# A conditional residual layer: which masks are expanded on the chip, who copies them, when GpSimd splits x, and the store of the last half batch

## What is computed

```python
masked_w = weight * mask[None, :, :]                  # weight [G, O, T], mask [O, T]
w_bot = jnp.einsum('bg,got->bot', y, masked_w)        # y = cond_8 [B, G]
out = x + jnp.einsum('bnt,bot->bno', x, w_bot) + bias
```

## Time and profile before

| | |
|---|---|
| Median of 3 runs | 73.07 us (73.03 to 74.49) |
| The profiled execution, its own time | 72.25 us |
| Its span, first to last instruction | 70.1 us |
| TensorE (PE) busy | 61.8 us, 88% of the span |
| VectorE (DVE) busy | 51.2 us, 73% |
| ScalarE (ACT) busy | 45.0 us, 64% |
| GpSimd (POOL) busy | 10.7 us, 15% |
| Moved by DMA | 20.20 MB, 288 GB/s over the span |

### The profile page before, as it was taken

One profiled execution on the slowest core, in us unless ns is written; L12 is line 12 of the kernel. 1 busy time (PEld: TensorE's weight loads), 2 busy tenths in 40 slices (PEclk: granted clock), 3 DMA queues, 4 the chain that ended last, 5 costly groups with the idle time before them and its releaser, 6 DMA issues.

```text
span 70.1 us, 1524 instructions
## 1 busy us (share of the span) xinstructions
PE 61.8 (88%) x666; PEld 57.7 (82%) x666; DVE 51.2 (73%) x34; ACT 45.0 (64%) x35; POOL 10.7 (15%) x16
## 2 busy tenths in 40 slices
PE   3997898847999973999999999999999999999910
PEld 3873786736988843999999999999999999999900
DVE  2207988938748999999993999999999199460040
ACT  3300476818579992049999999999922999504500
POOL 5400059980349000000000000000000000000000
PEclk9999999999999999999999999999999999999996
DMA  0999999999630003999899999999899721998383
GB/s 1 241 298 382 409 423 449 397 430 280 248 164 0 0 0 126 416 332 220 353 435 435 400 435 376 386 348 283 271 395 376 297 115 61 402 409 339 136 313 150
DMA packets 4901, 20.20 MB, mean 288 GB/s; under 512 B 544, under 2 KB 800, under 8 KB 3872
## 3 DMA queue, kind: packets, MB, share of 16 engines
q1 hardware_dynamic: 4752, 20.06, 76.3%
q10 hardware_dynamic: 144, 0.07, 0.4%
HBM read 11.73 MB, written 8.39 MB: 287 GB/s over the span
## 4 chain that ended last, share of the span: by engine, by line
PE 64%; DVE 18%; DMA 7%; issue 3%; SPq 2%; ACT 2%; ACTq 0%
PE slots L311 19%; PE slots L313 19%; PE slots L312 19%; DVE w_raw L452 7%; DMA weights<-in_weight 7%; PE slots L286 7%; DVE w_lo L436 5%; DVE x_lo L430 3%; DVE weights L423 2%; ACT w_hi L362 2%; SPq L157 1%; PE slots L277 1%; DVE weights L446 1%; SPq L154 1%; ACTq L380 0%
## 5 line engine op out<-in xcount | busy, mean ns | idle before, releaser
L311 PE MATMUL slots<-x_hi,w_hi 128*128 128x256 f32 x112 | 31.3, 280 | 1.6 <-DVE x_lo L430 1.6
L312 PE MATMUL slots<-x_lo,w_hi 128*128 128x256 f32 x112 | 31.3, 279 | 0.0
L313 PE MATMUL slots<-x_hi,w_lo 128*128 128x256 f32 x112 | 31.3, 279 | 0.0
L311 PEld LDWEIGHTS slots<-x_hi,w_hi 128*128 128x128 f32 x112 | 21.0, 188 | 1.9 <-issue 1.9
L312 PEld LDWEIGHTS slots<-x_lo,w_hi 128*128 128x128 f32 x112 | 21.0, 188 | 0.0
L313 PEld LDWEIGHTS slots<-x_hi,w_lo 128*128 128x128 f32 x112 | 21.0, 188 | 0.0
L436 DVE TENSOR_TENSOR w_lo<-w_raw,w_hi 128x2048 fp32r<-128x2048 f32 (+1 forms) x8 | 17.3, 2174 | 1.2 <-ACT w_hi L362 1.2
L430 DVE TENSOR_TENSOR x_lo<-x_ring,x_hi 128x2048 fp32r<-128x2048 f32 x7 | 16.0, 2286 | 2.9 <-ACT x_hi L356 2.7
L356 ACT CAST x_hi<-x_ring 128x2048 fp32r<-128x2048 f32 x6 | 11.4, 1906 | 6.5 <-DMA x_ring<-in_x 6.5
L371 ACT ACTIVATE weights<-slots,smalls 128x1024 f32<-128x1024 f32 x11 | 11.8, 1113 | 3.5 <-PE slots L313 3.5
L377 ACT COPY w_raw<-slots 128x1024 f32<-128x1024 f32 x8 | 8.0, 1013 | 9.3 <-PE slots L286 9.3
(11 more groups left out here) (21 smaller groups left out, 16.1 us busy)
## 6 DMA issues: line engine op xcount, KB each, us to landing
x_ring<-in_x SPq DMA_DIRECT2D x8, 1024.0 KB, 9.3
out<-weights SPq DMA_DIRECT2D x15, 512.0 KB, 6.0
weights<-in_weight SPq DMA_DIRECT2D x3, 512.0 KB, 6.4
x_ring<-in_mask SPq DMA_DIRECT2D x2, 512.0 KB, 6.4
weights<-in_weight SPq DMA_DIRECT2D x2, 256.0 KB, 3.9
out<-weights SPq DMA_DIRECT2D x2, 256.0 KB, 2.2
few_masks<-in_few SPq DMA_DIRECT2D x1, 128.0 KB, 2.4
smalls<-in_small ACTq DMA_DIRECT2D x1, 65.0 KB, 2.6
```

Of the source, the lines that this page charges most:

```text
L311: nc.tensor.matmul(dst, wh, xh, start=(k == 0), stop=False)
L312: nc.tensor.matmul(dst, wh, xl, start=False, stop=False)
L313: last = nc.tensor.matmul(dst, wl, xh, start=False, stop=(k == KC - 1))
```

## The change

- The repeated masks that the host sends are now those of chunks 0 and 3 (`REPEATED = (0, 3)`); the expanded ones are those of chunks 1 and 2. The amount of data is the same.
- ScalarE issues the two halves of mask 0, around `smalls`. SP's order becomes few, weights 0 (two halves), weights 1, 2, 3, mask 3, x of group 0.
- TensorE expands mask 1 first, mask 2 in the middle of unit 0. ScalarE copies each to SBUF (`mask_by_act`), and the multiplications of chunks 1 (VectorE) and 2 (GpSimd) read it there. All four masks lie in slots 1 and 2 of `x_ring`, so x of group 1 is loaded only after `masked_by_dve` of 3 and `masked_by_pool` of 1, x of group 2 after `masked_by_pool` of 2.
- VectorE masks chunk 1 after it has copied its slot of unit 0; ScalarE copies both slots of unit 1. Unit 1 waits for the second mask copy instead of for the masks of chunk 1; unit 2 still waits for those, but only behind its four identity matmuls.
- GpSimd makes x_hi of group 1 between its second and third gather; VectorE makes x_lo of group 1 ahead of its two halves of w_lo.
- The last half, (7, 1): its fourth sample goes to a PSUM bank of its own (`very_last`). Its columns 0 to 511 are finished by ScalarE after two samples, 512 to 767 by VectorE after three, 768 to 1023 by ScalarE at the end, which also issues that last store.

The core of the diff:

```diff
+REPEATED = (0, 3)
...
+        def mask_of(c):
+            return x_ring[:, 1 + (c in REPEATED), (c // 2) * SLOT:(c // 2 + 1) * SLOT]
...
+        def raw_act(u):
+            return u + 1 + (u >= 1)
+        def raw_dve(u):
+            return u + 1 - (u >= 1)
...
 (SyncE)
-            sp.dma_start(weights[:, 1, :], weight[1]).then_inc(chunk_loaded[0], 16)
-            for c in range(BY_SPREAD, CHUNKS):
-                sp.dma_start(masks[:, c - BY_SPREAD, :], mask[c - BY_SPREAD]).then_inc(chunk_loaded[c - 1], 16)
+            for c in range(1, CHUNKS):
                 sp.dma_start(weights[:, c, :], weight[c]).then_inc(chunk_loaded[c - 1], 16)
-            for g in range(XS - 1):
-                load_group(g)
-            sp.wait_ge(masked_by_pool, CHUNKS - BY_SPREAD)
-            load_group(XS - 1)
+            sp.dma_start(mask_of(CHUNKS - 1), mask[1]).then_inc(chunk_loaded[CHUNKS - 2], 16)
+            load_group(0)
+            sp.wait_ge(masked_by_dve, 3)
+            sp.wait_ge(masked_by_pool, 1)
+            load_group(1)
+            sp.wait_ge(masked_by_pool, 2)
+            load_group(2)
...
 (GpSimd)
+            pool.wait_ge(chunk_loaded[1], 16)
+            pool.wait_ge(mask_by_act, 2)
+            nc.gpsimd.tensor_tensor(weights[:, 2, :], weights[:, 2, :], mask_of(2), ALU.mult).then_inc(masked_by_pool, 1)
+            pool.wait_ge(chunk_loaded[2], 32)
+            nc.gpsimd.tensor_tensor(weights[:, 3, :], weights[:, 3, :], mask_of(3), ALU.mult).then_inc(masked_by_pool, 1)
...
+            gather(0, 0)
+            gather(0, 1)
             pool.wait_ge(x_loaded[1], 16)
             nc.gpsimd.tensor_copy(x_hi[:, 1, :], x_ring[:, 1, :]).then_inc(x_hi_first, 1)
+            gather(1, 0)
+            gather(1, 1)
...
 (TensorE, unit u)
-                if u == 1 or u == 2:
-                    pe.wait_ge(masked_by_dve, 3)
+                if u == 1:
+                    pe.wait_ge(mask_by_act, 2)
...
+                if u == 2:
+                    pe.wait_ge(masked_by_dve, 3)
...
                 for q in range(QU):
+                    if u == 0 and q == 2:
+                        pe.wait_ge(mask_by_act, 1)
+                        spread_mask(1)
...
+                        if g == GROUPS - 1 and h == 1 and b == NB - 1:
+                            pe.wait_ge(out0_by_act, g)
+                            dst = very_last
...
 (ScalarE)
+            act.dma_start(mask_of(0)[:, 0:BANK], mask[0, :, 0:BANK]).then_inc(first_loaded[0], 16)
             act.dma_start(smalls[:], small).then_inc(smalls_loaded, 16)
+            act.dma_start(mask_of(0)[:, BANK:SLOT], mask[0, :, BANK:SLOT]).then_inc(first_loaded[1], 16)
...
+            for n in range(BY_SPREAD):
+                act.wait_ge(mask_spread, n + 1)
+                nc.scalar.copy(mask_of(n + 1).rearrange("p (q t) -> p q t", t=T), few_wide[:, :, n, :]).then_inc(mask_by_act, 1)
             for u in range(UNITS):
                 act.wait_ge(unit_ready, 2 * u + 1)
                 nc.scalar.copy(raw_slot(u, 0), slots[:, 2 * (u % 2), :]).then_inc(raw_by_act, 1)
+                if u == 1:
+                    act.wait_ge(unit_ready, 2 * u + 2)
+                    nc.scalar.copy(raw_slot(u, 1), slots[:, 2 * (u % 2) + 1, :]).then_inc(raw_by_act, 1)
...
+            act.wait_ge(products_ready, HO * GROUPS)
+            nc.scalar.activation(result(GROUPS - 1, 1)[:, SLOT - N:SLOT], very_last, ACT.Identity,
+                                 bias=bias(1)).then_inc(last_by_act, 1)
+            act.wait_ge(last_by_act, 2)
+            act.dma_start(out[GROUPS - 1, 1, :, SLOT - N:SLOT], result(GROUPS - 1, 1)[:, SLOT - N:SLOT]
+                          ).then_inc(stored[SLOTS - 1], 16)
...
 (VectorE)
-                nc.vector.tensor_tensor(cols, cols, few_wide[:, 2 * h:2 * h + 2, 0, :], ALU.mult).then_inc(masked_by_dve, 1)
+                dve.wait_ge(first_loaded[h], 32)
+                cols = slice(h * BANK, (h + 1) * BANK)
+                nc.vector.tensor_tensor(weights[:, 0, cols], weights[:, 0, cols], mask_of(0)[:, cols],
+                                        ALU.mult).then_inc(masked_by_dve, 1)
...
             for u in range(UNITS):
+                if u == 1:
+                    dve.wait_ge(chunk_loaded[0], 16)
+                    dve.wait_ge(mask_by_act, 1)
+                    nc.vector.tensor_tensor(weights[:, 1, :], weights[:, 1, :], mask_of(1), ALU.mult).then_inc(masked_by_dve, 1)
+                else:
+                    dve.wait_ge(unit_ready, 2 * u + 2)
+                    nc.vector.tensor_copy(raw_slot(u, 1), slots[:, 2 * (u % 2) + 1, :]).then_inc(raw_by_dve, 1)
+            low_x(1)
             low_weights(1, 0, 2)
             low_weights(1, 2, 4)
-            low_x(1)
```

More of the change, by code:

```diff
@@ L118, in conditional_residual @@
         products_ready = sem("products_ready")
-        last_half_ready = sem("last_half_ready")
+        last_ready = sem("last_ready")
+        last_by_act = sem("last_by_act")
+        last_by_dve = sem("last_by_dve")
         out0_by_act = sem("out0_by_act")
@@ L185, in _ @@
             store(GROUPS - 1, 0)
[L186 to L191, removed]
+            sp.wait_ge(last_by_act, 1)
+            sp.dma_start(out[GROUPS - 1, 1, :, 0:BANK], result(GROUPS - 1, 1)[:, 0:BANK]).then_inc(stored[SLOTS - 1], 16)
+            sp.wait_ge(last_by_dve, 1)
+            sp.dma_start(out[GROUPS - 1, 1, :, BANK:BANK + N], result(GROUPS - 1, 1)[:, BANK:BANK + N]
+                         ).then_inc(stored[SLOTS - 1], 16)
             for s in range(SLOTS):
-                sp.wait_ge(stored[s], 16 * (HO * GROUPS // SLOTS + (s == SLOTS - 1)))
+                sp.wait_ge(stored[s], 16 * (HO * GROUPS // SLOTS + 2 * (s == SLOTS - 1)))
         @block.gpsimd
@@ L235, in _, with spread_mask @@
+            gather(0, 0)
+            gather(0, 1)
             pool.wait_ge(x_loaded[1], 16)
             nc.gpsimd.tensor_copy(x_hi[:, 1, :], x_ring[:, 1, :]).then_inc(x_hi_first, 1)
+            gather(1, 0)
+            gather(1, 1)
         @block.tensor
         def _(pe):
[L240 to L249, removed]
+            def spread_mask(n):
+                for i in range(TILES):
+                    rows = slice(i * ROWS, (i + 1) * ROWS)
+                    last = nc.tensor.matmul(few_wide[:, i, n, :],
+                                            spread[rows, n * R:(n + 1) * R, :].rearrange("p r g -> p (r g)"),
+                                            few_masks[rows, :], start=True, stop=True)
@@ L313, in multiply_group @@
                             last = nc.tensor.matmul(dst, wl, xh, start=False, stop=(k == KC - 1))
-                        if g == GROUPS - 1 and h == 1 and b == 1:
-                            last.then_inc(last_half_ready, 1)
+                        if g == GROUPS - 1 and h == 1 and b in (1, 2):
+                            last.then_inc(last_ready, 1)
                     last.then_inc(products_ready, 1)
@@ L362, in high_weights, with finish @@
                 nc.scalar.copy(part(w_hi, g, lo, hi), raw_part(g, lo, hi)).then_inc(w_hi_ready, 1)
-            def finish(g, h, done, cols=slice(0, SLOT)):
+            def finish(g, h, done):
                 j = 2 * g + h
@@ L437, in low_weights, with finish @@
                                         ALU.subtract).then_inc(w_lo_ready, 1)
-            def finish(g, cols=slice(0, SLOT)):
+            def finish(g):
                 j = 2 * g + 1
@@ L467, in _ @@
                     low_weights(g + RS)
-            finish(GROUPS - 1, slice(BANK, SLOT))
+            dve.wait_ge(last_ready, 2)
+            dve.wait_ge(stored[SLOTS - 1], 16 * (GROUPS // 2 - 1))
+            nc.vector.tensor_scalar(result(GROUPS - 1, 1)[:, BANK:BANK + N], product(GROUPS - 1, 1)[:, BANK:BANK + N], bias(1),
+                                    None, ALU.add).then_inc(last_by_dve, 1)
 def kernel(**inputs):
```

61 lines of the change are left out of this document (32 added, 29 removed).

## The result

The changed kernel is slower, by about 1.6%: 1.0159 times the kernel before, 95% interval 1.0102 to 1.0216 (medians 74.22 us, 73.89 to 76.23, against 73.62 us, 73.03 to 74.49). Measured again later (experiment 5), the ratio was 1.008 (1.002 to 1.014). Every ratio compares undisturbed executions only, the medians and ranges are of all, and the traces of experiments 1, 2 and 5 to 8 are of executions well above the fastest of their kernel, so of those only single starts, durations and gaps are used. The profiled execution took 74.19 us with a span of 72.4, against 72.25 and 70.1. I had forecast slower, at 75.4 us in a range of 72.2 to 76.6: the direction and the mechanism hold, the size was about twice too large.

A forecast was written before the change was run, and what follows sets the result against it. Before group 1 a chain of waits, largely VectorE's copies, was taken to set the pace, then TensorE. Terms: +3.4 - 0.45 - 0.4 = +2.5 us, 75.6 against the median of 73.07; given as 75.4, range 72.2 to 76.6.

The forecast's parts named there:

- The block on chunk 1's mask: Masks: GpSimd's mask of chunk 2 comes first, VectorE's of chunk 1 stands until 11.94, unit 2 starts 3.56 us later.
- the rival without contention: Masks and last gather: GpSimd doesn't block VectorE or the reverse; sum +0.1 us, 73.2 us; chance 12%.
- Unit 7 ends 3.4 us later: Masks and units before group 1: the delay of unit 2 carries through, so unit 7 ends at 22.2.
- 0.88 us of issue: Inside unit 5: a stretch where TensorE waits for nothing the profile shows, kept unchanged, bounds 0 and 0.88.
- From unit 7 to group 1: New x_hi and x_lo order: 1.5 us won ahead of group 1, 0.7 lost as x_lo blocks GpSimd's last gather.
- the much slower rival: Last gather of group 0: it must let x_lo and both w_lo halves pass, 2.3 us more, 77.7 us; chance 7%.
- Ahead of group 2: After group 0: group 2 waits 0.1 to 0.5 us for VectorE's x_lo and w_lo, taken as 0.35.
- The end: Last half: 256 columns on ScalarE and a 128 KB store win 0.4 us, bounds 0.1 and 0.6.
- The rival with VectorE first: Masks: VectorE masks chunk 1 before GpSimd's mask, which waits instead; sum 0, 73.1 us (72.0 to 74.0); chance 25%.

The follow-up runs named there:

- experiment 5: The changed kernel run again unaltered, with three other kernels on one chip; ratio to the kernel before 1.008 (1.002 to 1.014).
- experiment 1: The changed kernel with VectorE masking chunk 1 before it copies its slot of unit 0; ratio to the kernel before 0.9975 (0.983 to 1.012).
- experiment 2: The changed kernel with VectorE's old order for group 1, w_lo halves then x_lo; ratio to the kernel before 1.0381 (1.027 to 1.049).
- experiment 6: The kernel before with GpSimd's x_hi of group 1 between its gathers and VectorE's x_lo ahead of w_lo; ratio 0.9929 (0.986 to 0.9997).
- experiment 7: The kernel before with only GpSimd's x_hi of group 1 moved between its gathers; no ratio, times 71.30 to 75.37 us.
- experiment 8: The changed kernel with 8 instead of 5 pairs of dummy matmuls at the start; no ratio, six times of 72.01 to 75.93 us.
- experiment 3: The changed kernel with one more wait: GpSimd's first mask waits for VectorE's three; ratio to the kernel before 1.0071 (0.9996 to 1.0146).
- experiment 4: The kernel before with the changed end alone; ratio 0.9978 (0.987 to 1.009).
- experiment 9: The kernel before with x_hi of group 1 between the gathers, the changed end and x of group 7 loaded earlier; ratio 0.9956 (0.989 to 1.002).
- experiment 10: The changed kernel with chunk 1 masked before unit 0's copy, VectorE's old group 1 order and x of group 7 loaded earlier; ratio 0.9896 (0.983 to 0.997).
- experiment 11: Changed kernel: chunk 1 masked before unit 0's copy, old group 1 order, earlier group 7 load, VectorE copying its unit 1 slot; ratio 0.9922 (0.987 to 0.997).
- experiment 12: Changed kernel with GpSimd's first mask behind VectorE's, old group 1 order, earlier load of group 7's x; ratio 0.9798 (0.974 to 0.986), median 71.73 us.

## Why the prediction was right, and where its sizes were off

**The block on chunk 1's mask: right, to 0.2 us.** I had unit 0 end at 9.0, GpSimd first at 9.58, VectorE through at 13.15 and unit 2 at 13.20. Measured are 8.98, 9.55, 12.97 and 13.03. The masks of chunk 0 came at 5.39, the early end of my range. GpSimd's second mask was delayed to 15.20 (15.5). Experiments 1 and 3 show it from both sides: the same multiplication takes 1.23 us before GpSimd, and 1.22 with GpSimd made to wait. So the rival without contention is out. By the Trainium skill (SBUF — State Buffer, section "Who interferes with whom") the one that issues second blocks entirely; in the four pairs above (the two masks, the second mask behind VectorE's, the gather behind x_lo, w_lo behind the gather) the trace agrees, in both directions, but for some 0.15 us: GpSimd's end at 11.90 plus 1.22 would be 13.12, and VectorE ended at 12.97.

**"Unit 7 ends 3.4 us later": the term that failed.** It ended at 20.90, 2.1 later than 18.80. I kept the 0.88 us of issue, "since its neighbourhood keeps its pace". It didn't recur: units 4 and 5 ran from 15.62 to 18.15 without it, so unit 5 took 1.35 us from its first identity matmul, against 2.56 before. Of the 1.21 us between them 0.88 are the stretch, and most of the rest lies right behind it, where 0.61 us went by before unit 5 was done:

```profile
15.44 0.61 PE slots L286 x7
```

(The kernel before, the chain.) I had taken a stretch from one execution as fixed. In four other kernels whose masks and units are those of the kernel before, it is missing in three (experiments 4, 6 and 9) and is 0.28 us in one (experiment 7); in experiment 3 it is 0.35. In those four the units also began later than in the first trace. So whether the long wait ahead of unit 2 hid the cause, and what TensorE waits for in that stretch, no run shows.

**From unit 7 to group 1: right.** 7.7 instead of 8.6 us, so 0.9 won, where I had 1.5 - 0.7. The gather was blocked by x_lo and got in between x_lo and w_lo (the much slower rival is out). TensorE stood idle for 0.39 us, but group 0 took 7.81 us from its first to its last matmul (20.79 to 28.60) instead of 7.17, so the gather cost 0.64 us, near the 0.7.

**Ahead of group 2: right,** 0.45 us for 0.35 (the two starts of L339 at 33.69 and 34.49 are 0.8 apart, 0.35 without a wait).

**Ahead of group 7: missed,** 0.6 us; the forecast had no such term. x of group 3 is loaded when group 0 ends, which is now 2.75 us later (28.6 instead of 25.84), while group 1 starts only 1.2 us later. ScalarE's and VectorE's chain of splits hangs on that load, not on TensorE. All later splits are 2.8 to 3.2 us late, and the 0.7 us of slack that group 7 had (w_lo ready at 60.28, wanted at 61.0) are used up: 63.32 and 62.8.

```profile
57.99 2.29 DVE L436 TENSOR_TENSOR w_lo<-w_raw,w_hi 128x2048 fp32r<-128x2048 f32 x1
...
61.04 2.28 DVE L480 TENSOR_TENSOR w_lo<-w_raw,w_hi 128x2048 fp32r<-128x2048 f32 x1
```

(w_lo of group 7, before and changed.) It is not so in every execution. In the second trace of the changed kernel (experiment 5) group 1 started 1.4 us later still, and TensorE did not wait ahead of group 7; x of group 7 had landed 8.8 us after its issue, against 9.7 in the first. With x of group 7 loaded earlier, the chain is free of it (experiments 9 to 12).

**The end: right as a sum,** 0.5 for 0.4, with 0.15 of it inside the span and 0.3 outside.

The sum is 2.1 - 0.9 + 0.45 + 0.6 - 0.15 = 2.1 us of span (measured 2.3), and 1.94 us of time from profiled execution to profiled execution, where I had 2.5 (74.8 us forecast for it, 74.19 measured). Some of that nearness is luck: the 0.6 us that I had missed ahead of group 7 made up for half of the 1.3 that the term of unit 7 had too much. The ratio of 1.0159 makes it 1.2 us. Part of the difference is that the profiled execution of before was one of its best. Weights 1 landed at 6.93 us in it; in four kernels that have the same first loads, L423's counterpart began at 7.33, 8.38, 8.47 and 8.57, and TensorE waited up to 1.6 us for it. The changed kernel has no need of them before 10.1 us. That the kernel before loses time there in its own executions is an inference, since only one of them was traced.

The rival with VectorE first was not met in the two traces of the changed kernel (10.14 and 10.41 against 9.55), nor in the two others with the same order (10.67 against 9.81 in experiment 2, 9.82 against 9.72 in experiment 8), but run as experiment 3, where it gave 1.007, that is 73.6 us on 73.07; I had written 73.1.

## What to carry to other kernels

Before moving an operand from PSUM to SBUF for VectorE, look at what GpSimd does in those microseconds: in every pair of these runs in which VectorE had two SBUF inputs and GpSimd a multiplication, a copy or a cast from SBUF, the later one stood nearly still until the first was over. If they must overlap, let the one on the critical path go first, with a wait on the other if need be. The four executions with that wait had spans of 70.8 to 71.4 us, the faster ones of the changed kernel 71.3 to 72.4, and a part of that difference is a quicker start of unit 0 (experiment 3). And when a stage is shortened, ask which load hangs on its old end; the splits of groups 3 to 7 hung on the end of group 0, and showed it only at group 7.

## What the runs showed of the hardware

In four traces the granted clock fell to 0.50 behind a TensorE wait: 2.00 us ahead of unit 2 in experiment 5 (and some 3.3 us at the low clock), 1.62 us in experiment 9, 1.50 in experiment 6 and 0.99 in experiment 4. It did not fall behind 2.20 us in the first trace of the changed kernel, nor behind 2.74 us in experiment 8. So the length of the wait alone doesn't decide it, and what does, no run shows.

Where the wait ahead of unit 2 is 0.65 us (experiments 3 and 12), the mean clock was 0.994 to 1.000 in all ten executions. It was 0.977 in six of the changed kernel's twelve, and in two of the four of experiment 2, which ran on the same chip as experiment 3. The kernel before has such executions too.

Small matmuls ran at half their pace also where the granted clock shows 1.00: 96 of them in 5.60 us in experiment 2, and the 32 of unit 1 in 2.00 us in experiment 1, against 1.17 in the changed kernel. Why the two disagree is open.

So is why ScalarE could begin with x of group 3 some 4.8 to 5.0 us after its load was issued in ten traces, and only after 6.1 to 6.3 us in four (experiments 2, 7, 10 and 11), which are the four in which TensorE waited about 1 us ahead of group 3.
